# A conditioned sequence model: the generation stage without loops, its stores gathered, modulation's products behind the last chunk

## The reference, cut to what matters

```python
# layer 0: an adapter whose weights are generated from cond (16 x 64)
dWd = ((cond @ Wdd.T + bdd) * 0.1).reshape(B, 128, 256)     # Wdd, Wdu: 32768 x 64 each
dWu = ((cond @ Wdu.T + bdu) * 0.1).reshape(B, 256, 128)
down = relu(einsum('bld,bnd->bln', x, Wd + dWd) + bd)
x = x + einsum('bln,bdn->bld', down, Wu + dWu) + bu
# layer 1: layer norm, times weight, plus bias, plus tanh(cond @ lin_w.T + lin_b)
# layer 2: a transformer block with modulation
t = silu(cond @ W_t1.T + b_t1) @ W_t2.T + b_t2
g1, b1, g2, b2, a1, a2 = split(silu(t + side) @ W_c.T + b_c, 6)   # "modulation"
h = layernorm(x) * g1 + b1;  attention of 16 heads over h @ W_qkv.T;  x += (o @ W_o.T + b_o) * a1
h = layernorm(x) * g2 + b2;  x += (gelu(h @ W_f1.T + b_f1) @ W_f2.T + b_f2) * a2
# layer 3: RMS norm with scale (cond @ norm_w.T + 1), gated MLP, ternary output weights
```

## Time and profile before

| | us |
|---|---|
| median of 3 runs | 934.63 |
| lowest, highest | 933.69, 936.41 |
| the profiled execution | 935.74 |
| its span, first to last instruction | 933.9 |
| TensorE busy | 843.1 (90%) |
| VectorE busy | 565.4 (61%) |
| ScalarE busy | 510.9 (55%) |
| GpSimd busy | 231.2 (25%) |

### The profile page before, as it was taken

The page is one execution under the profiler, slowest core; times in us unless marked ns, Lnnn a source line. Parts: engine busy times, 40 slices in busy tenths (PEclk is TensorE's granted clock), DMA queues, the critical chain, the costliest instruction groups (busy, mean ns, idle before and its releaser), DMA issues.

```text
span 933.9 us, 15916 instructions
## 1 busy us (share of the span) xinstructions
PE 843.1 (90%) x5852; PEld 633.5 (68%) x5852; DVE 565.4 (61%) x1063; ACT 510.9 (55%) x796; POOL 231.2 (25%) x333
## 2 busy tenths in 40 slices
PE   6642577999999999999999999999999999999977
PEld 4101355687777778787878787878777777776665
DVE  1212586575757667575858585858485867656424
ACT  1101444565565657574748575656666574756542
POOL 1001204150405041323232231405050514130310
PEclk9855777999999999999999999999999999999998
DMA  9997643423161433324151515151424132320000
GB/s 344 365 366 252 248 138 124 148 80 122 62 203 38 135 97 114 120 78 156 47 187 47 188 47 188 46 173 61 154 76 142 65 127 80 104 80 25 24 12 12
DMA packets 58477, 118.48 MB, mean 127 GB/s; under 512 B 6336, under 2 KB 15936, under 8 KB 55696
## 3 DMA queue, kind: packets, MB, share of 16 engines
q1 hardware_dynamic: 58400, 117.48, 36.6%
HBM read 82.77 MB, written 34.16 MB: 125 GB/s over the span
## 4 chain that ended last, share of the span: by engine, by line
PE 74%; issue 9%; DMA 7%; DVE 4%; ACT 2%; SPq 2%; POOL 2%; POOLq 0%; DVEq 0%; ACTq 0%
PE bank L486 30%; PE bank L692 11%; PE pair_s L653 6%; PE pair_s L618 5%; PE pair_t L639 5%; PE pair_t L486 4%; DMA hyp<-in_hyper 3%; PE bank L737 3%; PE bank L664 3%; PE bank L567 2%; PE bank L729 1%; PE bank L561 1%; DVE oq L1145 1%; DMA wc<-in_cols 1%; PE bank L574 1%
## 5 line engine op out<-in xcount | busy, mean ns | idle before, releaser
L851 ACT ACTIVATE Pr<-pair_t 128x1024 f32<-128x1024 f32 x128 | 131.3, 1026 | 125.2 <-PE pair_t L639 121.5
L1121 DVE TENSOR_REDUCE nmax<-pair_s 128x4 f32<-128x1024 f32 x128 | 155.8, 1217 | 34.5 <-PE pair_s L618 33.9
L692 PE MATMUL bank<-wf,G 128*128 128x256 f32 x512 | 123.0, 387 | 0.1
L486 PE MATMUL bank<-wup_hi,hD_hi 128*128 128x512 f32 x256 | 109.4, 427 | 4.8 <-POOL hD_lo L1316 4.1
L1344 POOL TENSOR_TENSOR x<-x,xcr 128x512 f32<-128x512 f32 x16 | 20.5, 1281 | 358.1 <-DVE x L1179 358.1
L692 PEld LDWEIGHTS bank<-wf,G 128*128 128x128 f32 x512 | 93.3, 190 | 15.5 <-issue 0.2
L486 PE MATMUL bank<-wup_lo,hD_hi 128*128 128x512 f32 x256 | 102.0, 398 | 0.0
L486 PE MATMUL bank<-wup_hi,hD_lo 128*128 128x512 f32 x256 | 101.9, 398 | 0.0
L618 PE MATMUL pair_s<-Kp,Qp 64*128 64x256 f32 x512 | 66.1, 337 | 21.7 <-DVE nmax L1121 13.0
L895 ACT ACTIVATE gl<-bank,rsD 128x512 f32<-128x512 f32 x64 | 44.1, 689 | 63.6 <-PE bank L486 63.4
L1189 DVE SCALAR_TENSOR_TENSOR hd<-bank,rsD,gl 128x512 f32<-128x512 f32 x64 | 47.9, 748 | 46.2 <-PE bank L486 34.7
(11 more groups left out here) (177 smaller groups left out, 1879.5 us busy)
## 6 DMA issues: line engine op xcount, KB each, us to landing
hyp<-in_hyper SPq DMA_DIRECT2D x16, 1024.0 KB, 10.2
Qp<-qk_scratch SPq DMA_DIRECT2D x64, 256.0 KB, 3.7
Kp<-qk_scratch SPq DMA_DIRECT2D x64, 256.0 KB, 3.6
qk_scratch<-q_hi SPq DMA_DIRECT2D x16, 512.0 KB, 2.8
qk_scratch<-k_hi SPq DMA_DIRECT2D x16, 512.0 KB, 4.0
tC<-rows_scratch SPq DMA_DIRECT2D x16, 384.0 KB, 3.6
cur_scratch<-gen SPq DMA_DIRECT2D x16, 256.0 KB, 10.1
xT_t<-in_xT SPq DMA_DIRECT2D x16, 256.0 KB, 4.2
```

What stands on the lines that cost most here:

```text
L486: mm = pe.matmul(dst, l, r, start=first and i == 0, stop=last and i == 2)
L692: mm = pe.matmul(bank[5][:, r * D:(r + 1) * D], G[:, k, r * P:(r + 1) * P], wf2[:, k, :], start=k == 0, stop=k == FT - 1)
L851: act.activation(Pr[:, p % 4, :, :].rearrange("p a n -> p (a n)"), pair_t[:, :, :].rearrange("p a n -> p (a n)"), ACT.Exp, scale=DH ** -0. ...
L1121: dve.tensor_reduce(nmax[:, n % 2, :, p % GP, :], pair_s[:, :, :].rearrange("p a (r n) -> p a r n", r=RT), AX.X, ALU.max, negate=True).the ...
```

## The change

- The hardware loops of the generation are written out on all engines.
- The four copies of a pass are stored together, behind the loads of slots 0 to 2 of the next pass and ahead of that of slot 3. The store is four transfers, one for each quarter of the columns: 32 partitions with 8 KB each, to rows of 8 KB in `cur_scratch`, which has a new layout. The last pass is stored in two halves (32 partitions with 4 KB, four transfers each). One semaphore `pass_out` counts them, and a copy of pass i waits for all the stores of pass i - 1.
- The loads of `wc` and `wo` move from the first pass to behind the first stores; the second chunk is loaded ahead of `wt2`.
- mod, a12 and co are computed behind the last chunk. `tb` is stored, and `tA` loaded, when they are done.
- The query weights are asked for behind the store of `tb`. Their split comes behind A.down on ScalarE and behind A.ln on VectorE.
- `cur` of a batch comes in one transfer of 128 partitions in place of two of 64.
- Waits: GpSimd and ScalarE no longer wait for everything ahead of turn 0, and the statistics no longer wait for `prep`; ScalarE waits for `mod` at A.ht, TensorE for the whole preparation at W.qkv.

```diff
     "ACT": """
-        0: W.qkv A.down A.lnb A.ht A.q W.fa A.k A.v 1: A.down W.up A.lnb A.ht B.t0 B.t1 A.q B.t2 B.t3 B.t4 A.k B.t5 A.v B.t6 B.t7 2: A.down C.lnb C.ht
+        0: A.down W.qkv A.lnb A.ht A.q W.fa A.k A.v 1: A.down W.up A.lnb A.ht B.t0 B.t1 A.q B.t2 B.t3 B.t4 A.k B.t5 A.v B.t6 B.t7 2: A.down C.lnb C.ht
...
     "DVE": """
-        0: W.qkv A.up A.lna A.lng A.ln A.q A.cur A.k 1: A.up A.lna B.s0 A.lng B.s1 A.ln B.s2 B.s3 B.p0 B.m0 B.s4 B.s5 A.cur B.s6 B.s7 B.p1 W.fa B.m1
+        0: A.up A.lna A.lng A.ln W.qkv A.q A.cur A.k 1: A.up A.lna B.s0 A.lng B.s1 A.ln B.s2 B.s3 B.p0 B.m0 B.s4 B.s5 A.cur B.s6 B.s7 B.p1 W.fa B.m1
...
+            def store_chunks(i, first, last):
+
+                sp.wait_ge(gen_act, 2 * i + last // 2)
+                sp.wait_ge(gen_dve, 2 * i + last // 2)
+                for q in range(QTS):
+                    sp.dma_start(cur_scratch[:, 4 * i + q, first * HALF:last * HALF],
+                                 gen[2 * NB * q:2 * NB * (q + 1), first:last, :].rearrange("p s n -> p (s n)")).then_inc(pass_out, 16)
...
-            with sp.Fori(0, NCH // 4 - 1) as i:
-                for s in range(4):
-
-                    sp.wait_ge(hyp_mm, i * 4 + (s + 1))
-                    sp.dma_start(hyp[:, s, :], hyper[:, bass.ds((i + 1) * (4 * CHC) + s * CHC, CHC)]).then_inc(hyp_in[s], 16)
-                    generated(i, s)
+            for i in range(1, NCH // 4):
+                for s in range(3):
+                    sp.wait_ge(hyp_mm, 4 * (i - 1) + s + 1)
+                    load_chunk(i, s)
+                store_chunks(i - 1, 0, 4)
+                if i == 1:
+                    sp.dma_start(wc[:, :, :].rearrange("p k n -> p (k n)"), cols[:, 736:736 + KT * 6 * D]).then_inc(wc_in, 16)
+                    sp.dma_start(wo[:, :, :].rearrange("p k n -> p (k n)"), w_o).then_inc(wo_in, 16)
+                sp.wait_ge(hyp_mm, 4 * i)
+                load_chunk(i, 3)
...
             load_rows(0)
-            for s in range(4):
-                generated(NCH // 4 - 1, s)
-            sp.wait_ge(rows_out, 16)
-            for s in range(4):
-                sp.wait_ge(gen_out[s], 16 * (NCH // 4))
+            store_chunks(NCH // 4 - 1, 0, 2)
+            store_chunks(NCH // 4 - 1, 2, 4)
+            sp.wait_ge(pass_out, 64 * (NCH // 4) + 64)
             load_weights(0)
+            sp.wait_ge(prep, len(PREP))
+            sp.dma_start(rows_scratch, tb[:, 0:5, :]).then_inc(rows_out, 16)
             sp.dma_start(wqkv_raw[:, :], w_qkv).then_inc(wqkv_in, 16)
...
-            sp.wait_ge(prep, len(PREP))
+            sp.wait_ge(rows_out, 16)
+            load_tables(0)
             sp.dma_start(wf1_raw[:, :], w_f1).then_inc(wf1_in, 16)
...
-                if not isinstance(i, int):
-                    act.wait_ge(gen_out[s], i * 16)
-                act.wait_ge(hyp_mm, i * 4 + (s + 1))
+                if i:
+                    act.wait_ge(pass_out, 64 * i)
+                act.wait_ge(hyp_mm, 4 * i + s + 1)
...
-    cur_scratch = nc.dram_tensor("cur_scratch", (NCH, P, 2 * D), F32, kind="Internal").ap()
+    cur_scratch = nc.dram_tensor("cur_scratch", (2 * NB, NCH, 8 * D), F32, kind="Internal").ap()
```

More of the change, by code:

```diff
@@ L298, in cond_seq_kernel @@
         hyp_in = [sem(f"hyp_in{i}") for i in range(4)]
-        gen_out = [sem(f"gen_out{i}") for i in range(4)]
+        pass_out = sem("pass_out")
         hyp_mm, gen_act, gen_dve = sem("hyp_mm"), sem("gen_act"), sem("gen_dve")
@@ L501, in _ @@
             mm.then_inc(pre_pe, 1)
+            for m in range(KT):
+                mm = pe.matmul(bank[7][:, m * NB:(m + 1) * NB], c64[:, NB + 2 * D + m * P:NB + 2 * D + (m + 1) * P], c64[:, 0:NB], start=True, stop=True)
+            mm.then_inc(pre_pe, 1)
             pe.wait_ge(cond_in, 32)
             generate(0, 0)
+            generate(0, 1)
             pe.wait_ge(wt2_in, 16)
-            pe.wait_ge(prep, PREP.index("s1") + 1)
+            pe.wait_ge(prep, made("s1"))
             for m in range(KT):
@@ L509, in _ @@
             mm.then_inc(pre_pe, 1)
-            generate(0, 1)
-            pe.wait_ge(wc_in, 16)
-            pe.wait_ge(prep, PREP.index("s2") + 1)
-            for m in range(8):
-                for k in range(KT):
-                    mm = pe.matmul(bank[6][:, m * NB:(m + 1) * NB], wc[:, k, m * P:(m + 1) * P], s2[:, k, :], start=k == 0, stop=k == KT - 1)
-            mm.then_inc(pre_pe, 1)
-            for m in range(KT):
-                mm = pe.matmul(bank[7][:, m * NB:(m + 1) * NB], c64[:, NB + 2 * D + m * P:NB + 2 * D + (m + 1) * P], c64[:, 0:NB], start=True, stop=True)
@@ L519, in _ @@
-            mm.then_inc(pre_pe, 1)
-            pe.matmul(bank[4][0:NB, 0:D], c64[:, 0:NB], c64[:, NB + D:NB + 2 * D], start=True, stop=True).then_inc(pre_pe, 1)
-            for k in range(KT):
-                mm = pe.matmul(bank[5][0:NB, 0:2 * D], s2[:, k, :], wc[:, k, 4 * D:6 * D], start=k == 0, stop=k == KT - 1)
-            mm.then_inc(pre_pe, 1)
-            generate(0, 2)
-            pe.wait_ge(wo_in, 16)
-            pe.wait_ge(small_in, 16)
-            pe.wait_ge(prep, PREP.index("mod") + 1)
@@ L528, in _, with modulation @@
-            for k in range(KT):
-                mm = pe.matmul(bank[6][0:NB, 0:D], bv[:, k:k + 1].to_broadcast([P, NB]), wo[:, k, :], start=k == 0, stop=k == KT - 1)
-            mm.then_inc(pre_pe, 1)
-            generate(0, 3)
-            with pe.Fori(1, NCH // 4) as i:
+            pe.matmul(bank[4][0:NB, 0:D], c64[:, 0:NB], c64[:, NB + D:NB + 2 * D], start=True, stop=True).then_inc(pre_pe, 1)
+            generate(0, 2)
+            generate(0, 3)
+            def modulation():
+                pe.wait_ge(wc_in, 16)
+                pe.wait_ge(prep, made("scale3"))
+                for m in range(8):
+                    for k in range(KT):
+                        mm = pe.matmul(bank[6][:, m * NB:(m + 1) * NB], wc[:, k, m * P:(m + 1) * P], s2[:, k, :], start=k == 0, stop=k == KT - 1)
+                mm.then_inc(pre_pe, 1)
+                for k in range(KT):
+                    mm = pe.matmul(bank[5][0:NB, 0:2 * D], s2[:, k, :], wc[:, k, 4 * D:6 * D], start=k == 0, stop=k == KT - 1)
+                mm.then_inc(pre_pe, 1)
+                pe.wait_ge(wo_in, 16)
+                pe.wait_ge(small_in, 16)
+                for k in range(KT):
+                    mm = pe.matmul(bank[7][0:NB, 0:D], bv[:, k:k + 1].to_broadcast([P, NB]), wo[:, k, :], start=k == 0, stop=k == KT - 1)
+                mm.then_inc(pre_pe, 1)
@@ L533, in _ @@
+            for i in range(1, NCH // 4):
                 for s in range(4):
                     generate(i, s)
-            pe.wait_ge(prep, len(PREP))
+            modulation()
             def with_qkv():
                 pe.wait_ge(dve_w, at(DVE_W, "qkv", 0))
+                pe.wait_ge(prep, len(PREP))
             def with_f1():
@@ L1272, in _ @@
             pool.memset(Va[:, :, :, :, DH:2 * DH], 1.0).then_inc(zero, 1)
[L1273 to L1276 removed]
+            pool.wait_ge(row_in, 48)
             pool.wait_ge(zero, 7)
```

114 lines of the change are left out of this document (52 added, 62 removed).

## The result

The changed kernel takes 938.48 us (median) against 934.5 for the kernel before: the ratio is 1.0044, 95% interval 1.003 to 1.0059. So it is slower by 0.3 to 0.6%. One of its 18 executions took 4065.86 us, for a reason that isn't known, and is not in the ratio. The profiled execution took 938.68 us, its span is 936.9, 3.0 more than before.

What follows compares the result with a forecast made beforehand. The generation's byte stream bounds the kernel before about 66 us, TensorE after the norm of batch 0; +3.4 us up to T and +1.5 behind it made +4.9, so 939.5 us like the median, range 930 to 943.5.

Steps and rivals of the forecast that it cites:

- T: Landing of the generation's last chunk, 61.66 us before; time lost there reaches the kernel's end one for one.
- Part 1: Generation's first pass: the 27 to 31 us gap in the load stream closes with modulation moved away, 2.9 us saved.
- Part 2: Generation's stores in four transfers of 32 partitions: 4.6 us a pass instead of 2.5, three passes, 6.3 us lost.
- Sum up to T: Stream gap closed (-2.9) plus slower stores (+6.3): last chunk lands 3.4 us later, ends -2.9 and +8.
- Part 3: Modulation computed behind the last chunk, up to batch 0's norm: 3.1 us saved to 1.5 lost, 1.5 lost taken.
- hidden both: Query weights' split, 1.5 us on VectorE and about as much on ScalarE, claimed hidden beside other steps, cost 0.
- The turns, 0: Later turns: one transfer for cur instead of two saves SP 0.6 us, TensorE is full, so no change.
- A: Rival: the generation's stores run at the full rate, so -1.4 us in all, 933.2 us; chance 0.27.
- B: Rival: stores at full rate and the clock high in modulation, so -7.0 us, 927.6 us; chance 0.10.
- C: Rival: slow stores but a high clock behind T, +3.4 - 3.5 = 0, 934.5 us; chance 0.07.

## Why the prediction was right

The direction, the size (939.5, measured 938.48) and most steps held. That the number came so close is partly luck. The sum had +4.9 us, the medians say +4.0: T is 0.5 us less late than it said, GpSimd's 1.5 us are missing from it, and so are the 2.6 us that the turns give back.

- **Part 1, the gap closes, 2.9 us saved:** right. The stretches from 14 us to the first pass's stores run at 426 and 420 GB/s. With one store of 128 partitions for a pass T is 1.6 us ahead of before. Two terms account for the other 1.3: the rate of 413 in place of 422 up to T there (0.7 us), and a store more ahead of the last chunk (0.6, see the sum).
- **Part 2, 6.3 us for the stores:** right in kind, too large. From 26 to 64.51 us the rate is 377 where 422 was possible: 45 x 38.5 = 1.73 MB, 4.1 us. Of these 3.5 lie in the three stretches with the stores (1.2, 1.0 and 1.3) and 0.6 outside them. A pass took 3.5 to 3.8 us, not 4.6, by this estimate; 1.05 MB in that time are 275 to 300 GB/s, where I had taken 230 from two rows in which 64 partitions were read. The Trainium skill, SBUF — State Buffer, section "Door 1: The DMA port swizzle (why [64,N] ≈ [32,N])", has about 218 GB/s as the limit from 32 partitions. The four stores together were above it; whether the loads behind them filled in isn't shown. What the step missed is that the loss depends on the order of the four: in the other order the same transfers cost 0.8 us in one kernel and 0.2 in the other, by the mean rates up to T (412 and 420). And the direction rested on less than the prediction thought: by its own sum a pass of 3.5 to 3.8 us makes the kernel 1.6 to 2.5 us slower, not the 2.8 that it called the least it could tell from no change.
- **Sum up to T:** predicted +3.4, measured +2.9. Two terms were missing on the way. The prediction counted three passes of stores ahead of the last chunk in both kernels; before, the twelfth store was issued behind it (52.10 against 51.38), so 22.5 MB stood ahead (16 chunks of 1.05 MB, 2.9 of stores, 2.8 of the rest), and 22.7 in the changed kernel: 0.6 us. And by then more had moved than stood ahead: before 371 GB/s x 61.66 us = 22.9 MB, in the changed kernel 367 x 64.51 = 23.7. So some 0.5 MB more of what is queued behind the chunk (base_t, xT, x) moved ahead of its end, 1.3 us of the stream. -2.9 + 4.1 + 0.6 + 1.3 = +3.1, an estimate from rounded rates.
- **Part 3, 1.5 us lost behind T:** right, by the chain it named. Modulation's 16 products took 7.01 us as in the earlier trace rows, the products ended at T + 12.8 (13.4 to 14.2 said), the tables were ready at T + 14.1, and the gate's sum, bound by tA, started at T + 23.0 (22.5 to 24 said) against T + 21.6: 1.4.
- **The split of the query weights "hidden both":** wrong as a statement; the price at the end isn't settled. ScalarE's part was hidden. VectorE's part held GpSimd's small sum, and GpSimd is on the chain there: 1.5 us at the transposes which the prediction had at 0. I looked for idle time on VectorE and didn't ask what runs on GpSimd at that moment. The run that took it away moved the gate by 1.0 us the other way, and its last x0 is only 0.2 us earlier.
- **The turns, 0:** wrong. One transfer for cur in place of two is worth 2.6 us by the medians of four and eighteen executions, 2.0 by the ratios, and 2.6 by the two places in the traces. "TensorE is full there" was read from 300 to 600 us; turn 4 lies ahead of that stretch, and there TensorE waited behind SP's row of issues.
- **Rivals:** A and B, the full rate, fell with the first stretch of stores (340 GB/s). The kernel with its quarters in the other order is at 933.8, where A said 933.2; the agreement says little, since A lacks the same terms as the forecast. C, the fast clock behind T, came in part: the granted clock was 0.50 through the 16-column products and 1.00 from 76 us on, but the tables bound, so it gave nothing.

The last x0's lag by terms, as measured: 2.9 to T, 1.4 to the gate and 1.5 for GpSimd are the 5.8 at the transposes of batch 0. The x0 of turn 1 is 6.3 late; where the 0.5 comes from isn't known. Then 0.9 are given back by turn 2 and 1.7 between turns 4 and 5, where the kernels with two transfers for cur give back little (0.2 and 0.7 at most), and 0.3 in small steps: 3.4 at the last x0, and 4.0 in the medians.

## What to carry to other kernels

When transfers touch few partitions, put neighbours in a queue on different halves of the partitions (0 to 63, 64 to 127): one line of order was worth 4.7 us here. Small work that has to be done once fits into the idle time of a streaming stage in blocks shorter than one chunk's idle time; in one piece it makes a gap ahead of the end of the stream or lies on the path behind it. Before calling a moved step hidden, look at what the other engines do in that time. Count the issues on a single issuing engine as work: one issue in the row decided whether TensorE waited in turn 4.
